# A decoder layer on one core: attention over heads by batched 128x128 products instead of elementwise products, with other orders and lags of the engines

## The reference

```
q, k, v = x Wq^T, x Wk^T, x Wv^T                 each seen as [n, head 16, token 64, 8]
att[n, token, i, j] = softmax_j(q_i . k_j / sqrt(8))   for each token, over its own 16 heads
out[n, head, token, :] = sum_j att v_j;  reshaped without a transpose to [n, 64, 128], Wo, bo
x = norm(x + out)
x = norm(x + retention(x, ctx, ctx))             16 heads, rotated q and k, decay, causal
x = norm(x + ffn(x))                             8 experts, inner width 512, the best 2 of each token
```

## Time and profile before

| | us |
|---|---|
| median of three runs | 1031.27 |
| lowest, highest | 1027.26, 1034.76 |
| profiled execution, its own span | 1027.0 |
| TensorE busy (share) | 839.8 (82%) |
| VectorE busy | 794.7 (77%) |
| GpSimd busy | 654.8 (64%) |
| ScalarE busy | 607.7 (59%) |
| last place computed, end of stage A's routing | 630.2 |

### The profile page before, as it was taken

How to read it: one execution, slowest core, us unless ns; L and a number is a source line. 1 busy time by engine, 2 the same in 40 slices (tenths; PEclk the granted TensorE clock), 3 DMA queues, 4 the chain that set the end, 5 groups by cost and what they waited for, 6 DMA issues and landing times.

```text
span 1027.0 us, 35115 instructions
## 1 busy us (share of the span) xinstructions
PE 839.8 (82%) x12164; PEld 639.6 (62%) x12164; DVE 794.7 (77%) x2219; ACT 607.7 (59%) x1416; POOL 654.8 (64%) x738
## 2 busy tenths in 40 slices
PE   1667699999999999989979770699999999999600
PEld 1445466666666666656655440599899999999500
DVE  4787899998988989878856642588888888888575
ACT  1123457667667777666766851466666666666355
POOL 0338776699989999988997456044444444444443
PEclk9687899999999999999998965799999999999855
DMA  9312122122232231212222002222222222222186
GB/s 307 79 27 48 35 52 54 36 66 67 47 72 52 65 68 50 65 37 60 47 50 63 23 22 63 66 64 61 61 63 65 65 62 64 63 61 59 45 257 222
DMA packets 145303, 72.72 MB, mean 71 GB/s; under 512 B 75024, under 2 KB 134544, under 8 KB 145136
## 3 DMA queue, kind: packets, MB, share of 16 engines
q1 hardware_dynamic: 124800, 40.56, 17.1%
q0 software_dynamic: 8640, 17.84, 5.2%
q10 hardware_dynamic: 11696, 12.08, 3.6%
HBM read 42.11 MB, written 28.34 MB: 69 GB/s over the span
## 4 chain that ended last, share of the span: by engine, by line
PE 33%; POOL 28%; issue 11%; DVE 3%; DMA 2%; another core or an unknown queue 1%; ACT 1%; POOLq 0%; SPq 0%; DVEq 0%; ACTq 0%
POOL prod_ev L1551 14%; POOL routed_rows L1568 9%; PE QKV L773 9%; PE ST L773 9%; PE XT L801 5%; PE SC L801 5%; POOL rs L1531 3%; DMA prod_ev<-token_halves 1%; DMA routed_rows<-xe,pos 1%; PE YY L589 1%; POOL frs L1613 1%; PE YY L791 1%; PE TR L791 1%; PE SC L562 1%
## 5 line engine op out<-in xcount | busy, mean ns | idle before, releaser
L1551 POOL TENSOR_TENSOR prod_ev<-e_sb,q_v 128x512 f32<-128x512 f32 x256 | 300.3, 1206 | 77.5 <-PE YY L589 40.1
L1600 POOL DMA_INDIRECT token_halves<-w_new,tok_i x142 | 137.9, 971 | 32.5 <-issue 22.2
L1568 POOL DMA_INDIRECT routed_rows<-xe,pos x128 | 131.2, 1025 | 30.4 <-issue 30.0
L1151 DVE TENSOR_TENSOR prod_qk<-q_v,QKV 128x2048 f32<-128x2048 f32 x64 | 145.4, 2274 | 4.9 <-ACT q_v L870 4.9
L1453 DVE TENSOR_TENSOR prod_ev<-prod_qk,prod_ev 128x1024 f16<-128x1024 f32 x71 | 87.0, 1225 | 56.1 <-ACT prod_ev L1028 31.1
L773 PE MATMUL QKV<-k_t,w_hl 128*128 128x256 f16 x852 | 117.2, 274 | 0.0
L773 PE MATMUL ST<-k_t,w_hl 128*128 128x256 f16 x852 | 116.9, 274 | 0.0
L411 POOL TENSOR_TENSOR marks<-half_c 128x1 f32<-128x1 f32 x103 | 19.7, 192 | 149.7 <-DVE w_new L1469 149.1
L1037 ACT ACTIVATE prod_qk<-QKV,silu_scale 128x512 f32<-128x512 f32 x142 | 90.0, 683 | 41.3 <-PE QKV L773 41.3
L1028 ACT CAST prod_ev<-prod_qk 128x1024 f16<-128x1024 f32 x71 | 74.2, 1045 | 62.9 <-DVE prod_qk L1479 62.9
L1479 DVE SCALAR_TENSOR_TENSOR prod_qk<-ST,hid_scale,prod_qk 128x512 f32<-128x512 f32 x142 | 99.5, 742 | 2.9 <-PE ST L773 1.8
(11 more groups left out here) (171 smaller groups left out, 1785.9 us busy)
## 6 DMA issues: line engine op xcount, KB each, us to landing
w_new<-routed_rows SPq DMA_DIRECT2D x71, 130.0 KB
prod_ev<-token_halves SPq DMA_DIRECT2D x16, 512.0 KB, 4.9
x_sb<-x SPq DMA_DIRECT2D x32, 128.0 KB, 2.8
x_res<-x SPq DMA_DIRECT2D x128, 32.0 KB
head_rows<-o_n SPq DMA_DIRECT2D x32, 128.0 KB
o_t<-head_rows SPq DMA_DIRECT2D x64, 64.0 KB
ctx_sb<-ctx SPq DMA_DIRECT2D x32, 128.0 KB
out<-prod_qk ACTq DMA_DIRECT2D x16, 256.0 KB, 4.0
```

The lines of the kernel that those rows point to most:

```text
L1151: eng.tensor_tensor(prod_qk[:, u, :, :].rearrange("p d (i j) -> p d i j", j=NH), q.unsqueeze(3).to_broadcast([P, HD, NH, NH]), k.unsqueeze ...
L1551: ins = eng.tensor_tensor(prod_ev[:, u, q, :, :, 0:HD], e_sb[:, it.slot(2), u, 64 * q:64 * q + 64].rearrange("p (i j) -> p j i", j=4).unsq ...
L1568: eng.indirect_dma_start(out=xs, out_offset=bass.IndirectOffsetOnAxis(ap=pos[:, r, 2 * u + k:2 * u + k + 1], axis=0), in_=xe[:, r, u, k, : ...
L1600: eng.indirect_dma_start(out=halves, out_offset=bass.IndirectOffsetOnAxis(ap=tok_i[:, s, u:u + 1], axis=0), in_=yw[:, s, u, :], in_offset= ...
```

## The change

Stages B and C stay as they are, but for the names of the buffers they share with stage A (and one small instruction beside each expert tile's scatter, which goes). Stage A gets another attention, other lags (TensorE 6, ScalarE 7, VectorE 6, GpSimd 6, SP 2) and another order in each engine's step.

- The host hands over x and ctx in another layout: x already transposed, [channel, 256 tokens] a duo; ctx transposed, the same with its channels exchanged in pairs, and once more in rows with zeros between, 1,024 columns a duo instead of 256.
- TensorE projects 128 tokens (the even ones, then the odd ones) in one product each. ScalarE copies the result into `qkv_sb` [128 tokens, 16, 64], whose 64 columns are q, 0, 0, q (for one parity or the other), k and v, 16 or 8 columns each.
- SP writes these 512 KB to DRAM and loads them back so that 8 token pairs x 16 channels lie in the partitions: `q_in` in one load, `k_own` and `v_own` in eight loads each, which put each token pair's block on the diagonal of a matrix that is otherwise zero.
- The scores of 256 tokens are then 16 products; VectorE takes the maximum over j inside a partition, subtracts it; TensorE transposes; ScalarE takes the exponential; 16 products with `v_own` give sums and denominators; VectorE divides; 8 products transpose the result. The second trip to DRAM and the second load of x are gone.
- The keys' rotation moves from VectorE to GpSimd, and is done in the transposed layout without TensorE.
- Small ones: both copies of a normed row in one ScalarE instruction, one exponential instead of four for the routing weights, one instruction for the one-hot rows, the placeholders `stand` gone.

The core of the diff:

```diff
-    PE_LAGS, ACT_LAGS, DVE_LAGS, POOL_LAGS, SP_LAGS = 13, 13, 14, 11, 9
+    X_RING, CTX_RING, Q_RING = 7, 3, 3
...
+            def heads_away(it):
+                r = it.slot(RING)
+                wait(it, qkv_ready[0])
+                wait(it, qkv_ready[1])
+                wait_ring(it, q_back, RING)
...
+                eng.dma_start(heads[r], qkv_sb[:, it.slot(2), :, :]).then_inc(heads_out[r], 16)
+            def queries_back(it):
+                r, s = it.slot(RING), it.slot(Q_RING)
+                wait_ring(it, heads_out)
+                wait(it, score_done, Q_RING)
+                eng.dma_start(q_in[:, s, :, :], heads[r].rearrange("(g a) x c -> (a x) g c", a=HD)[:, :, 0:2 * NH]
+                              ).then_inc(q_back[s], 16)
+            def keys_back(it):
+                r, s = it.slot(RING), it.slot(2)
+                wait_ring(it, heads_out)
+                wait(it, score_done, 2)
...
+                for a in range(HD):
+                    eng.dma_start(k_own[NH * a:NH * a + NH, s, :, NH * a:NH * a + NH],
+                                  heads[r].rearrange("(g a) x c -> a x g c", a=HD)[a, :, :, 2 * NH:3 * NH]).then_inc(k_back[s], 16)
...
+                for a in range(HD):
+                    eng.dma_start(v_own[NH * a:NH * a + NH, s, :, a, 0:2 * HD],
+                                  heads[r].rearrange("(g a) x c -> a x g c", a=HD)[a, :, :, 3 * NH:4 * NH]).then_inc(v_back[s], 16)
...
+            def step(at, s):
+                if it := at(0):
+                    load_tokens(it)
+                if it := at(1):
+                    heads_away(it)
...
+                if it := at(2):
+                    load_context(it)
...
+            def scores(it):
+                wait_ring(it, q_back)
+                wait_ring(it, k_back, per=P)
+                wait_last(it, n_duo, (e_ready, 1), (sub_ready, 1))
+                for w in range(4):
+                    for c in range(4):
+                        mm = eng.matmul(SC[QUARTER * c:QUARTER * c + QUARTER, P * w:P * w + P],
+                                        q_in[:, it.slot(Q_RING), 4 * w + c, :], k_own[:, it.slot(2), 4 * w + c, :],
+                                        start=True, stop=True)
...
+            def ret_scores(it, u):
+                wait(it, q8_ready)
+                wait(it, kt_ready)
...
```

More of the change, by code:

```diff
@@ L171, in wait_ring, with run_duos @@
 def wait_ring(item, sems, back=0, per=16):
-    if item.i is None and item.off - back < 0:
+    if item.i is None:
+        n = item.off - back
+        if n >= 0:
+            item.eng.wait_ge(sems[n % len(sems)], (n // len(sems) + 1) * per)
         return
     item.eng.wait_ge(sems[(item.off - back) % RING], item.ring_count(per, back))
+def run_duos(eng, n, lags, body):
+    for s in range(n + lags):
+        body(lambda lag: Item(eng, None, None, s - lag) if 0 <= s - lag < n else None, s)
 def run_steps(eng, n, first, lags, body):
@@ L726, in step @@
+            def step(at, s):
+                if it := at(0):
+                    project(it, 0)
+                if it := at(3):
+                    residual(it)
+                if s == 1:
+                    spread_max(0)
+                if it := at(2):
+                    scores_across(it)
+                if it := at(4):
                     ret_scores(it, 1)
                 if it := at(0):
-                    tokens_across(it)
-                if it := at(5):
-                    sums(it, 0)
+                    project(it, 1)
+                if it := at(2):
+                    values(it)
+                if it := at(4):
+                    ret_scores(it, 0)
+                if it := at(1):
+                    scores(it)
+                if it := at(5):
+                    rows_across(it)
+                if it := at(6):
+                    ranks(it)
+                if it := at(4):
+                    ret_values(it)
+                if s == 1:
+                    spread_max(1)
+                if it := at(2):
+                    heads_across(it)
+                if it := at(5):
+                    gates(it)
@@ L1101, in moments @@
                 wait(it, nb_ready, 2 - NORM_GAP * norm)
-                stand(it, norm)
                 slot = norm_slot(None, it) if norm else it.slot(2)
@@ L1262, in top_values @@
                 wait(it, lg_ready)
-                wait(it, ex_ready, 2)
-                stand(it, 2)
+                wait(it, df_ready, 2)
                 for u in range(2):
@@ new lines, in step @@
+                if it := at(1):
+                    divide(it)
+                if it := at(3):
+                    mask(it, 0)
+                if it := at(5):
+                    gate_weights(it)
+                if it := at(5):
+                    places(it)
+                if s == 1:
+                    low_weights(1)
+                if it := at(2):
+                    queries_by_sin(it)
+                if it := at(5):
+                    counts(it)
+                if it := at(2):
+                    queries_by_cos(it)
```

894 lines of the change are left out of this document (396 added, 498 removed).

## The result

The changed kernel takes **1004.02 us** (median of 4 runs, 997.79 to 1005.9) against 1033.01 us for the kernel before (4 runs, 1027.26 to 1038.48): a ratio of 0.973, 95% interval 0.967 to 0.978. It is faster, as forecast, but by 29 us where 93 were forecast, and 1004 lies just above the range. The profiled execution took 1002.46 us with a span of 1000.6 us.

What follows compares the result with a forecast made beforehand. GpSimd was taken to bound the kernel before, SP's queue after, at 14.2 us a duo: 67 + 412 + 58 = 537 us to the last place, plus 397 unchanged and 4 to the median, 938 us; range 885 to 1000 us.

Steps and rivals of the forecast that it cites:

- GpSimd bounds the kernel before: Stage A's steady run: GpSimd sets the 15.8 us period; the change takes its eight products, 9.4 us a duo.
- gone from the chain: Sign in the profile after: GpSimd under 60% busy in stage A and no longer in the chain of waits.
- SP's queue sets the period: Stage A: 17 load issues behind one round trip make 14.2 us a duo; case 914 to 976 us, chance 0.50.
- a rival only: Slower than before: loads back on SP's queue from 0.69 us each; 1135 us at 0.9 us a load; chance 0.10.
- The wait for the write: SP's queue: from the context's issue to the first load back 0.8 + 4.3 + 0.4 = 5.5 us.
- The ends of stage A: Third duo's maximum at 67 us; 58 us from the last duo's maximum to the last place, at 537 us.
- the bound of 914 us: Lower end of the forecast case, SP's queue at 13.5 to 15.5 us a duo, 914 to 976 us.
- The engines' own loop: Stage A's hard loop round the engines, from one maximum's subtraction to the next: 12.3 to 12.6 us a duo.
- that rival's 12.4 to 13.5: Engines set stage A's period if loads issue in 0.41 us or less: 889 to 918 us, chance 0.19.
- The rival "between": Stage A at 15.5 to 17.2 us: TensorE loses clock, or transfers and scatters obstruct each other before the write lands; chance 0.15.
- TensorE idle before the scores: Sign in the profile after: TensorE stands idle ahead of the scores, waiting for a transfer.
- The rule on many small transfers: SP's loads back: skill page says join small transfers; 17 fixed parts one after another, 34 us a duo; chance 0.01.

Runs made afterwards that it cites:

- e4: Four of the eight key loads of each duo left out, against the changed kernel: 929.72 us, one run.
- e15: Each key load issued as two halves, eight issues more on SP's queue, against the changed kernel: 1209.06 us, ratio 1.173.
- e12: e10 with four of the eight value loads issued by ScalarE, ahead of residual in its step: 921.81 us, ratio 0.896.
- e13: e11 with all eight value loads moved within ScalarE's step, to ahead of residual: 920.25 us, ratio 0.892.
- e5: TensorE computes each duo's 16 score products twice, against the changed kernel: 1002.5 us, ratio 0.975.
- e10: e8 with the token load issued one step earlier against everything else of SP's step: 950.84 us, ratio 0.924.
- e8: e1 with GpSimd's scatters also held until TensorE has done ret_values of its current step: 952.42 us, ratio 0.927.
- e1: SP issues the heads' write ahead of tokens and context, against the changed kernel: median 994.12 us, ratio 0.968; two shorter runs 983.5 and 988.0.
- e3: Values' eight loads issued by ScalarE at the end of its step instead of SP, against the changed kernel: 1007.64 us, ratio 0.979.
- e11: e10 with the eight value loads on ScalarE at the end of its step, scatters held: 1003.88 us, ratio 0.975.

## Why the prediction was right or wrong, point by point

- **GpSimd bounds the kernel before; without its products it is no bound.** Right: 159 us busy of 375 (42%, under 60%). That it would be gone from the chain was wrong in the letter: the chain follows it through its wait for the context. TensorE's work came out as summed, 293.5 / 375 x 16.2 = 12.7 us a duo.
- **SP's queue sets the period.** Right in the mechanism, e4 and e15 show it. **The failed step is its size, 14.2 us where it is 16.2 to 16.5.** Against its terms: the loads back 10.1 us instead of 17 x 0.50 = 8.5 (+1.6); from the context's issue to the first load back 1.0 + 5.1 = 6.1 instead of 5.5 (+0.6); the rest 0.3 instead of 0.2. In the loads the typical issue was priced rightly (0.448 and 0.047 between two). Missing are two things that a median doesn't show. The first key load of a duo takes 1.2 us, not 0.45, behind the queries' load. And about once a duo another issue takes 1.1 to 1.9 us, which adds 1.0 us a duo in the mean. I had seen the row that says so, the gather's 359/475/**1337**, and used the median for the sum and the maximum for a rival only. 29 x 2.03 = 59 of the 66 us are here.
- **The wait for the write.** I let the last byte be followed by 0.4 us; and write, context and tokens together took 6.1 us, not 5.5. This is the smaller part.
- **The ends of stage A.** The third maximum came at 75.6 us, not 67: +8.6 us. The tail from the last maximum to the last place was priced at 58 us and is 56.6. The rest, 397, is 397.6. Sum of all: 934 + 8.6 + 59 - 1.4 + 0.6 = 1001, the span. Why the third maximum came later, no run was made to show. Two sums were rough: the bound of 914 us leaves out the 4 us that its partner 976 has, and the queries' data entered with 2.0 us where 2.5 had been worked out; neither changes a case.
- **The engines' own loop, 12.3 to 12.6 us.** Not seen in the changed kernel. In e12 and e13, where by the waits it comes forward, it is 13.5 and 13.6, at the upper end of that rival's 12.4 to 13.5. By its own sum that is 67 + 29 x 13.5 + 58 + 401 = 918 us, and e13 took 920; that the two agree so well is in part luck, since e13's third maximum came 8 us late (74.8 us) and what lies behind its last one was 5 us shorter than 58 + 397. My tour round one step went through the second residual but not through the buffer that residual has to share with it.
- **The rival "between", 976 to 1020 us,** holds the time and not for its reasons. The clock fell to 0.85, but e5 adds products to the changed kernel, and e10 takes TensorE's waits for tokens and much of the lost clock from e8 (0.97 for 0.91), both at no change. Before the write lands, the transfers in each other's way are worth the 0.6 us above and no more.
- **TensorE idle before the scores**: wrong in place. It stands 3 us a duo at project for tokens, and 0.4 before the scores (its weight loads there 1.3).
- **The rule on many small transfers.** The Trainium skill's page "DMA: Bandwidth & Descriptors", section "Rules for kernel authors", was the voice against; taken literally it would have been over 1,600 us. The fixed part of about 2.0 us, which I set against SP's loads, stands on that page of the Trainium skill for transfers that GpSimd issues. The rule's direction is borne out: four small loads less are worth 74 us (e4). The price that the trace shows is 0.5 us of the issuing queue each, nothing like a whole fixed part.
- **What no step had**: a slowed ret_values. It costs nothing in the changed kernel, but whoever had followed my diagnosis and mended SP's order alone would have found 18 us instead of 52.

Not settled: why the first key load is long (2.6 us where the context is issued just ahead of the queries' load, 1.2 where it is not); the long issues, which no run took away (apart from the first key loads, all 23 of them between 100 and 500 us coincide in the trace with a transfer of the instruction queue, 0.9 us in the median and 1.4 at most); and by what way the scatters slow TensorE.

## What to carry to other kernels

A faster set of engines is worth nothing if the change leaves a serial queue with 20 issues in its place: sum the queue in means, not medians, since one issue in seventeen at three times the price is a tenth of the time. Move DMA issues to where an engine waits anyway, and not ahead of what others wait for (84 us here for the same eight issues, the clock's part in it not told apart). When a cure of a sure bound brings nothing, look in its trace for an operation that has grown without a wait; a second effect has come forward.

## What the runs showed of the hardware that I had not expected

- 32 records of small products (128x32 weights, 128 columns) take 1.1 us alone and 3.6 to 5.4 us where GpSimd issues four indirect scatters at the same time; no semaphore shows, only "issue" (e1, e3). Holding the scatters back by one wait was worth 33 us (e1's shorter runs to e8).
- A DMA issue on ScalarE's queue holds back the activations that stand behind it (2.9 us idle in e11), but where activations are already let go it runs beside them (e13: the eight scalings take 3.0 us with seven issues beside them, and 3.0 without in e11).
- The issue of a strided load costs its queue 0.448 us in one form and 0.675 in another of half the bytes (e15): its price does not follow the bytes.
